# 68 filler transposes instead of 44, and separate storage for the last two chunks' scaled one-hot rows

## What is computed

```
x = x + xattn(ctx, layernorm(x))      # in-projection, causal conv, silu, selective scan over L
x = x + ffn(layernorm(x))             # router + 64 experts + shared expert

xattn: u = silu(conv(ctx @ in_proj)); dt, Bm, Cm = projections of u
       state = state * exp(dt * A) + dt * u * Bm;  y = sum_n state * Cm
       out = (y + D * u) * silu(z)
ffn:   scores = softmax(x @ gate.T);  top 6 of 64 experts per token
       y = sum over chosen experts of score * (silu(x Wg) * (x Wu)) Wd
       shared = (silu(x Sg) * (x Su)) Sd
```

## Time and profile before

| | us |
|---|---|
| three executions: median (lowest to highest) | 1032.78 (1031.4 to 1037.14) |
| the profiled execution, its own time | 1031.32 |
| its span in the profile | 1029.6 |
| the 44 filler transposes | from 596.62, 4.97 long |
| first transposes of `xn` of the last sequence | 604.04 |
| first gather for the experts | 631.89 |
| `tokens(0)`, begin of the expert phase on PE | 637.91 |

### The profile page before, as it was taken

How to read it: one execution, slowest core, us unless ns; L and a number is a source line. 1 busy time by engine, 2 the same in 40 slices (tenths; PEclk the granted TensorE clock), 3 DMA queues, 4 the chain that set the end, 5 groups by cost and what they waited for, 6 DMA issues and landing times.

```text
span 1029.6 us, 12583 instructions
## 1 busy us (share of the span) xinstructions
PE 860.5 (84%) x4213; PEld 479.6 (47%) x4213; DVE 603.9 (59%) x862; ACT 498.0 (48%) x895; POOL 565.4 (55%) x318
## 2 busy tenths in 40 slices
PE   6375656667999786999789988999999988999984
PEld 3153445455455374545555474444444443444431
DVE  4589899889888988998798853222122211111111
ACT  4589545797776788766766223222122211221210
POOL 0387998987988988979777601122222212213111
PEclk9568655589899988999899979999999999999998
DMA  8633344334434553333637675999999999999995
GB/s 284 231 123 123 125 159 147 123 123 166 129 123 144 176 165 117 123 123 104 224 111 241 226 274 208 402 394 386 399 395 388 398 397 396 396 386 399 387 387 137
DMA packets 68411, 250.66 MB, mean 243 GB/s; under 512 B 10506, under 2 KB 13078, under 8 KB 68092
## 3 DMA queue, kind: packets, MB, share of 16 engines
q1 hardware_dynamic: 54740, 226.09, 58.4%
q0 software_dynamic: 7712, 18.88, 7.5%
q10 hardware_dynamic: 5896, 4.90, 1.5%
HBM read 230.67 MB, written 19.17 MB: 243 GB/s over the span
## 4 chain that ended last, share of the span: by engine, by line
PE 51%; DVE 16%; DMA 10%; issue 6%; ACT 6%; SPq 3%; POOL 2%; POOLq 0%; ACTq 0%; DVEq 0%
PE ps L683 13%; PE ps L886 10%; PE ps L678 9%; PE ps L694 8%; PE ps L910 6%; DVE ps L1272 6%; DMA arena<-in_L_ffn_w_down 5%; DVE arena L1279 4%; SPq L569 3%; DVE arena L1298 2%; ACT ps L1081 2%; PE ps L919 1%; DMA out_rows<-routes,idxs 1%; DVE arena L1272 1%; DMA out_rows<-xn,idxs 1%
## 5 line engine op out<-in xcount | busy, mean ns | idle before, releaser
L1516 POOL TENSOR_TENSOR arena<-arena 128x1024 f32<-128x1024 f32 x128 | 300.0, 2359 | 57.2 <-DMA arena<-bc_rows 40.0
L678 PE MATMUL ps<-ident,arena 128*128 128x128 f32 (+2 forms) x1408 | 238.5, 321 | 84.5 <-DVE ps L1280 39.8
L678 PEld LDWEIGHTS ps<-ident,arena 128*128 128x128 f32 (+2 forms) x1408 | 199.3, 177 | 190.1 <-issue 85.8
L1081 ACT ACTIVATE ps<-arena,An 128x511 f32<-128x511 f32 x256 | 165.2, 680 | 109.5 <-DVE ps L1280 93.4
L1272 DVE TENSOR_TENSOR_SCAN ps<-ps,arena 128x1024 f32<-128x1024 f32 x82 | 187.6, 2287 | 15.5 <-ACT ps L1081 14.7
L886 PE MATMUL ps<-arena 128*64 128x352 f32 x984 | 158.7, 461 | 7.7 <-issue 3.9
L683 PE MATMUL ps<-xnT,sw 128*128 128x512 f32 x320 | 152.1, 619 | 12.7 <-ACT arena L1042 11.8
L1530 POOL DMA_INDIRECT arena<-xn_rows,idu x32 | 34.1, 1066 | 208.6 <-DVE wcol L1426 149.1
L1521 POOL TENSOR_TENSOR arena<-arena 128x1024 f32<-128x1024 f32 x46 | 108.4, 2356 | 49.0 <-DVE arena L1272 49.0
L1433 DVE TENSOR_TENSOR arena<-arena,ps 128x352 f32<-128x352 f32 x32 | 16.7, 522 | 171.1 <-PE ps L886 171.1
L886 PEld LDWEIGHTS ps<-arena 128*64 128x64 f32 x984 | 73.2, 137 | 80.8 <-issue 71.3
(11 more groups left out here) (166 smaller groups left out, 903.6 us busy)
## 6 DMA issues: line engine op xcount, KB each, us to landing
arena<-bc_rows SPq DMA_DIRECT2D x128, 512.0 KB, 4.8
arena<-in_L_ffn_w_down SPq DMA_DIRECT2D x59, 768.0 KB, 23.0
arena<-in_L_ffn_w_gate SPq DMA_DIRECT2D x64, 704.0 KB, 23.5
arena<-in_L_ffn_w_up SPq DMA_DIRECT2D x59, 704.0 KB, 23.3
arena<-in_x SPq DMA_DIRECT2D x4, 1024.0 KB, 6.8
xn_rows<-xn ACTq DMA_DIRECT2D x4, 1024.0 KB, 6.4
out_rows<-arena SPq DMA_DIRECT2D x4, 1024.0 KB, 5.2
extra<-in_L_ffn_w_up SPq DMA_DIRECT2D x5, 704.0 KB, 22.3
```

The source lines that it names most:

```text
L678: return nc.tensor.matmul(dst, src, ident[0:k, 0:k], is_transpose=True, **kw)
L1081: a = nc.scalar.activation(ps[:, 2 * (c % 2) + n, 1:L], dt[k][:, 1:L], ACT.Exp, scale=An[:, k, NB * g + n:NB * g + n + 1])
L1516: G.tensor_tensor(R[c % RING], dtu[k][:, None, :].to_broadcast([P, NB, L]), Brep[n % REPS], ALU.mult)\
```

## The change

`TAILFILL` becomes 68. A second view, `late_ids`, is laid into the arena behind the 20 weight slots, over words that held sequence 2's rows (`xb`) and that later hold the gathered tokens `xg`. Chunks 14 and 15 (the last two) use it in place of `ohsid`, on ACT, DVE and PE. For these two chunks ACT and DVE no longer wait on `tab_mm` but on `out_st`, the landing of all four stores of `x` rows from the arena to the output. On DVE the first two chunks of the last sequence now carry a wait on `tab_mm` (that the table matmuls of chunks 10 and 11, of the sequence before, are done).

```diff
-TAILFILL = 44
+TAILFILL = 68
@@
         at[0] = ASLOTS * SLOT
+        late_ids = arena[:, at[0]:at[0] + half].bitcast(BF16).rearrange("p (j k a e) -> p j k a e", j=2, k=K, a=2)
@@
+        def ids_of(i):
+            return (ohsid if i < NC - 2 else late_ids)[:, i % 2]
@@
-                        mm = nc.tensor.matmul(ps[:, bank, 0:E], ohsid[:, i % 2, k].rearrange("p a e -> p (a e)"),
+                        mm = nc.tensor.matmul(ps[:, bank, 0:E], ids_of(i)[:, k].rearrange("p a e -> p (a e)"),
@@
-                    if i >= 2:
+                    if i >= NC - 2:
+                        act.wait_ge(s["out_st"], 16 * B)
+                    elif i >= 2:
                         act.wait_ge(s["tab_mm"], i - 1)
                     for n, f in enumerate((pcol[:], float(i + 1))):
                         if n == 0 or b < B - 1:
-                            nc.scalar.activation(ohsid[:, i % 2, :, n, :], ohs[:, c], ACT.Copy, scale=f)\
+                            nc.scalar.activation(ids_of(i)[:, :, n, :], ohs[:, c], ACT.Copy, scale=f)\
@@
                     dve.wait_ge(s["ohs_ready"], i + 1)
                     if c >= 2:
+                        dve.wait_ge(s["out_st"], 16 * B)
+                    else:
                         dve.wait_ge(s["tab_mm"], i - 1)
                     with nc.allow_low_precision("whole numbers up to 16, exact"):
-                        V.tensor_scalar(ohsid[:, i % 2, :, 1, :], ohs[:, c], float(i + 1), None, ALU.mult)\
+                        V.tensor_scalar(ids_of(i)[:, :, 1, :], ohs[:, c], float(i + 1), None, ALU.mult)\
```

## The result

| | kernel before | changed kernel |
|---|---|---|
| median of 19 executions each, us | 1032.78 (1027.42 to 1037.14) | 1026.25 (1024.73 to 1029.95) |
| ratio, 95% interval | | 0.9952 (0.9936 to 0.9967) |
| the profiled execution, us | 1031.32 | 1029.95 |
| its span, us | 1029.6 | 1028.2 |

The medians lie 6.5 us apart, the ratio says 5.0 (0.48%, so 0.5% lies within its interval), and the two profiled executions differ by 1.4. The times of the kernel before fall into two groups, six from 1027.4 to 1028.9 and thirteen from 1030.5 to 1037.1, and its median lies in the upper one; that is why the medians lie further apart than the ratio says.

What follows compares the result with a forecast made beforehand. Weight streaming fixes the expert phase's length, so PE's half-clock tail before `tokens(0)` counts: 5.7 (filler) + 0.9 (own place) = 6.6, cut to 5.9 by the scores' landing. Forecast 1026 us, between 1025.4 and 1026.9; range 1023 to 1031.5.

Steps and rivals of the forecast that it cites:

- The filler: PE in the tail: 24 more transposes close the 2.45 us pause and keep 2.4 GHz, gaining 5.7 us up to `pos`.
- Its price of 0.26: Before `xn`'s transposes: the longer filler frees PE at 604.30, 0.26 us behind the 604.04 at which `xnT` began.
- Logits: Logits and transposes on PE: at full clock they end at 610.5 instead of 614.33, a gain of 3.8 us.
- The halved `pospre`: `pospre` on PE, 1.61 us: between no gain and half, the prediction took half, a gain of 0.8.
- The own place: Table of the last chunks: without the wait for PE's table matmuls, the indices gain 0.9 us.
- What is late next: Gather's wait for the scores in HBM: they land at about 627.1 behind `xn`'s packets, cutting 6.6 us gained to 5.9.
- The size: Whole kernel: `tokens(0)` moves from 637.91 to 632.0, so 5.9 us off the time.
- A microsecond gained before `tokens(0)` should be a microsecond of the whole: Expert phase: it streams weights without a break, so it ends earlier by as much as it starts earlier.
- A: Rival, logits in the tail: the clock falls anyway, only 0.6 us gained, 1030.7; chance 0.15.
- B: Rival, scores' store: it still lands at 630.2, so 2.9 us gained, 1028.4; chance 0.13.
- C: Rival, filler: its 68 transposes run at half clock, ending at 612.0, 7.1 us slower, 1038.4; chance 0.03.
- D: Rival, gather: scores land by 626, PE's chain binds and 6.6 us are gained, 1024.7; chance 0.14.

Runs made afterwards that it cites:

- e1: The kernel before with 68 filler transposes instead of 44, the last two chunks left in their old places; median 1026.75 us, ratio 0.9957.
- e5: The changed kernel with the last sequence's scores stored from POOL's queue instead of ACT's; median 1026.91 us, ratio 0.9955.
- e8: The kernel before, unchanged, run again for a second profile; profiled execution 1028.15 us.
- e9: The changed kernel, unchanged, run again for a second profile; median 1026.02 us, ratio 0.9948.
- e3: The changed kernel with 18 more identity transposes while PE waits for the gather and 6 behind tokens(0); median 1026.25 us, ratio 0.9949.
- e12: The changed kernel with 56 filler transposes instead of 68; median 1026.86 us, ratio 0.9967.
- e6: The changed kernel with 20 identity transposes while PE waits for the last but one pair's down weights; median 1027.29 us, ratio 0.9957.
- e7: The changed kernel with scores stored by POOL and 20 transposes before the last but one pair's down passes; median 1023.81 us, ratio 0.9924.
- e10: The same kernel as e7, run again; median 1026.6 us, ratio 0.9962.

## Why the prediction was right, and where it was not

**The filler (right).** Ending near 604.30 was foretold, measured 604.14. Its price of 0.26 did not appear: `xnT` began at 603.97, 7.4 us behind the filler's start in both kernels. Logits: foretold end 610.5, measured 610.4. `pos`: 613.0 against 612.88. The halved `pospre`, a choice between two bounds, took 0.7 (610.44 to 611.16) where I had 0.8, so a little less than the lower bound.

**The own place (right in its size, and worth nothing beside the filler).** The indices came at 624.13, foretold 624.4. e1 shows that they may come 1.1 later without anything else moving. The prediction had said that the gather would be last by 0.7, and cut 6.6 to 5.9 for it, but still counted the 0.9 as part of the sum. By its own numbers ACT's copy would have ended at 632.2 without the own place, 0.2 behind the 632.0 that the gather set, so its sum held 0.2 of the 0.9. Taken alone the filler gives the same.

**What is late next (right in the sum, wrong in the reason).** The scores landed at 627.4, foretold 627.1, and the gather began 1.06 behind that. `tokens(0)` came at 632.44, foretold 632.0. e5 confirms that the scores' landing is what held it. But the prediction let the scores' packets begin only behind the end of `xn`, at 620 in place of 623.1, and take 6 us as before. In the traces the first of them comes 3.5 us behind the issue in all eleven profiles with the store on ACT's queue, whether `xn`'s had ended or not: at 623.28 for an issue at 619.73 before, at 619.28 for one at 615.79 in the changed kernel, where the last of `xn`'s came at 620.18. So the start moved by the whole 4.0, and what kept the landing from following is that the 512 packets now took 7.6 us from first to last, against 6.35. The first packet came 0.7 earlier than foretold and the landing 8.2 behind it in place of 7.1, so that the landing fits to 0.3 is partly luck. Why the same packets took longer is open.

**The size (right for the profile it was built on, too large in the mean).** The prediction took 5.9 from a kernel before whose low clock lasted 13.6 us, and got 5.5 against it. It did not ask how long the low clock lasts in other executions. e8 shows 6.8 us of it; against that the change is worth 2.3 (39.7 against 37.4). Between 2.3 and 5.4 lies the mean of 4.7. The forecast of 1026 rested on a base between the profiled run and the median. That it met the median of 1026.25 to 0.25 is luck: its step of 5.9 is above the ratio's 5.0, and its base below the median.

**"A microsecond gained before `tokens(0)` should be a microsecond of the whole" (right on the average, wrong for one execution).** Of 5.5 us at `tokens(0)` 4.0 were left at the first refill, since the clock fell at 634.9, behind a pause that the change itself makes longer: PE's passes end earlier and the gather does not follow as far. The first slot was foretold free near 636.5 and was refilled at 638.4. No rival had this; the prediction named it only among the signs of being wrong, as a clock lost at other places. At the end 1.4 were left. From the first gate matmul to the end, 14 profiles took between 389.3 and 394.3 us, and the first profile of the changed kernel was the longest of them; e9, the same kernel, took 389.7, and its execution was 5.7 us shorter than the profiled one of the kernel before. Waits for weights late in the phase fall together with low clocks in varying number (from 634 to 1015 four falls in the changed kernel's first profile, one each in e3 and e9). That these make the whole of the 5 us is not shown.

**The rivals.** A (the clock falls among the logits) did not happen in any of eight profiles with 68 transposes. My doubt that the kernel before "may have kept it" in some executions was not borne out either: it fell in each of three profiles, but for different lengths. B (the scores land no earlier) fell with the landing at 627.4; while the prefetch ran, 512 packets of 256 bytes were slow, but they got through. C (the filler at half clock) did not happen: the 68 ran at 7.59/68 = 0.112 us each. D (the gather not last) did not happen either; e5 brings it about, and there `tokens(0)` comes 6.8 us earlier than in the kernel before's first profile (34.5 against 41.3), where D had 6.6.

## What to carry to other kernels

A pause of an engine on the critical path can cost more behind it than in it: 2.45 us of idle PE cost another 2.3 to 5.4, and filler for the pause is cheap as long as it ends with it. When a chain is shortened, find what stood just behind it, here a store of 128 KB in 512 packets of 256 bytes: it decides how much of the next microsecond is kept. When a transfer lands sooner on another queue, read from its packets whether it started sooner or ran in fewer pieces, before the order of the queue gets the credit. One profile is one execution; before building a sum on a low-clock stretch, see whether a second profile shows it as long.

## What the runs showed of the hardware that was not expected

- The same pause, in the same kernel, was followed by 6.8 us at 0.50 in one profile and by 13.6 in two. PE's records were without a gap in both.
- 1.14 us of pause kept the clock in one profile, 2.45 lost it in four of four. The wait for the gather, 2.05 us and then 0.75 behind four transposes, lost it in one profile, and 2.08 to 2.27 with the same 0.75 kept it in three (e9, e12, e6).
- The same 128 KB store, rows of 256 bytes to HBM, went as 512 packets over 7.6 us from ACT's queue, and as 32 packets of 4096 bytes within 0.6 to 0.7 us from POOL's (e5, and the same in e7 and e10). From issue to landing it took 11.5 us (e1) and 5.7 (e5).
- The scan phase, the same in all kernels, ended at 596 to 597 us in most profiles, at 594.9 in one and at 600.6 in another. That alone makes some of the 10 us over which the kernel before spreads.
